# Down projection of expert tiles as three products of rounded parts, and table writes in bursts, in a perceiver layer with 64 experts

## The reference

```python
g = silu(einsum('ech,eih->eci', buf, expert_wg))
u = einsum('ech,eih->eci', buf, expert_wu)
out_buf = einsum('eci,ehi->ech', g * u, expert_wd)   # the down projection, i = 256, h = 512
rows = out_buf[e_flat, pos]
routed = (rows.reshape(T, K, h) * topw[..., None]).sum(1)
```

## Time and profile before

| | us |
|---|---|
| median of 3 runs | 1292.07 (1289.84 to 1292.19) |
| the profiled execution | 1291.37 |
| its span, first to last instruction | 1289.4 |
| TensorE busy in the span | 1225.0 (95%) |
| VectorE, ScalarE, GpSimd busy | 733.9, 594.8, 395.2 |
| stage B's item loop | from about 772 to 1268 |

### The profile page before, as it was taken

The page is one execution under the profiler, slowest core; times in us unless marked ns, Lnnn a source line. Parts: engine busy times, 40 slices in busy tenths (PEclk is TensorE's granted clock), DMA queues, the critical chain, the costliest instruction groups (busy, mean ns, idle before and its releaser), DMA issues. The chain is left out here.

```text
span 1289.4 us, 31822 instructions
## 1 busy us (share of the span) xinstructions
PE 1225.0 (95%) x9830; PEld 923.9 (72%) x9831; DVE 733.9 (57%) x1509; ACT 594.8 (46%) x1184; POOL 395.2 (31%) x312
## 2 busy tenths in 40 slices
PE   5999999999999999999999789999999999999993
PEld 4887788787887887877786347766777676667661
DVE  4445665756656657566557746556555556655550
ACT  2453433433434434333342165566655656656551
POOL 0002012021021120210202324566554656756442
PEclk9999999999999999999999999999999999999997
DMA  6732110210201102101012277999999999999886
GB/s 223 288 117 45 51 37 19 69 36 12 76 19 50 38 19 69 36 19 58 13 50 68 74 264 252 314 314 342 302 297 283 308 330 333 347 283 317 260 236 106
DMA packets 67370, 205.44 MB, mean 159 GB/s; under 512 B 16064, under 2 KB 18496, under 8 KB 56913
## 3 DMA queue, kind: packets, MB, share of 16 engines
q1 hardware_dynamic: 43392, 159.78, 34.3%
q0 software_dynamic: 23888, 44.40, 16.5%
HBM read 177.32 MB, written 37.03 MB: 166 GB/s over the span
## 5 line engine op out<-in xcount | busy, mean ns | idle before, releaser
L982 PE MATMUL bank<-ch,wkh 128*128 128x256 f32 x512 | 157.2, 307 | 11.9 <-DVE cl L660 8.4
L566 ACT ACTIVATE kt<-bank,colb 128x256 f32<-128x256 f32 x128 | 60.7, 474 | 225.7 <-PE bank L984 225.7
L459 POOL TENSOR_TENSOR rstd<-vep,half 128x1 f32<-128x1 f32 x32 | 20.7, 647 | 462.2 <-DVE vep L641 462.2
L1650 PE MATMUL ebank<-guh,xth 128*128 128x512 f32 x380 | 154.8, 407 | 1.5 <-DVE xtl L1548 0.8
L1543 DVE TENSOR_TENSOR gul<-wgu,guh 128x2048 fp32r<-128x2048 f32 x54 | 123.8, 2293 | 56.9 <-ACT guh L1459 56.8
L1387 POOL DMA_INDIRECT xg<-xn_rows,ig x95 | 123.4, 1299 | 89.8 <-issue 64.7
L1652 PE MATMUL ebank<-guh,xtl 128*128 128x512 f32 x380 | 149.0, 392 | 0.0
L1651 PE MATMUL ebank<-gul,xth 128*128 128x512 f32 x380 | 148.3, 390 | 0.0
L983 PE MATMUL bank<-cl,wkh 128*128 128x256 f32 x512 | 145.0, 283 | 0.0
L984 PE MATMUL bank<-ch,wkl 128*128 128x256 f32 x512 | 144.9, 283 | 0.0
L1680 PE MATMUL ebank<-wd,ht 128*128 128x512 f32 x292 | 134.3, 593 | 0.8 <-ACT ht L1444 0.8
(11 more groups left out here) (242 smaller groups left out, 2466.5 us busy)
## 6 DMA issues: line engine op xcount, KB each, us to landing
wgu<-in_egu SPq DMA_DIRECT2D x54, 1024.0 KB, 8.7
wd<-in_edn SPq DMA_DIRECT2D x54, 512.0 KB, 6.5
sgu<-in_egu SPq DMA_DIRECT2D x17, 1024.0 KB, 9.0
craw<-in_ctx SPq DMA_DIRECT2D x32, 514.0 KB, 3.3
sdn<-in_edn SPq DMA_DIRECT2D x17, 512.0 KB, 5.7
wqkv<-in_wqkv SPq DMA_DIRECT2D x1, 3072.0 KB, 18.1
second_sums<-x1b SPq DMA_DIRECT2D x9, 256.0 KB, 3.9
xa<-in_x SPq DMA_DIRECT2D x8, 256.0 KB, 3.0
```

Source lines behind the costliest of these rows:

```text
L982: mm(out, wkh[:, c, w], h[:, c, :], start=c == 0, stop=False)
L1650: mm(out, ah[:, c, :], bh[:, c, :], start=c == 0, stop=False)
```

## The change

In stage B the down projection is done with rounded parts too, over all of its 256 inner columns (`DS = 2` chunks of 128, which is all of `IC`).

- ScalarE's copy of the turned h (L1444) now rounds it (`hth`), and VectorE makes its remainder (`low_h`, 128x256), first thing in its step after the index copies.
- ScalarE rounds the down weights of item k (`high_d`, 128x1024) in step k between silu of k and the x cast of k+2; VectorE makes their remainder (`low_d`, 128x1024) at the end of step k, behind the gate-up remainder. Both have two buffers.
- TensorE's `down` waits for `d_low` and `hT_low` and does six products per tile instead of two plain ones.
- The turned h of the shared expert and a small scratch row move into buffers that exist already, and ScalarE waits once more ahead of its loop.

In stage A the eight table writes of a tile go one behind the other without pacing, ScalarE's passes are written out instead of looped, and 28 semaphore increments (`FILL`) stand at the end of its stage. The name `FILL` had held the value that closes masked scores; all of the mask is open here.

```diff
@@ -83,8 +83,7 @@
 KEEP = 3
 EARLY = K
 WRITE = 8
-PACE = ("v", "A3", "DEN1", "NUM1")
-PACED = K - 1 - len(PACE)
+FILL = 28
 
 
 def place(n, t):
@@ -476,7 +475,6 @@
                 if front and s == WRITE:
                     table_ready(t - 2)
                 if front and WRITE <= s < WRITE + K:
-                    wait(pool, s_kv, 6 * (BT * t + b) + k, tick)
                     write(s - WRITE)
 
             def on_pre(n, t):
@@ -511,18 +509,12 @@
                     pool.wait_ge(s_nb, NB)
                     residual(t + 1)
                 if n == "outproj":
-                    if type(t) is int and t == NT - 1:
-                        px_wait(pool, n, t)
-                        write(K - 1)
                     root(norm_post(t, 1))
                     root(norm_post(t, 2))
                 if n == "pos" and type(t) is int and t >= NT - 2:
                     table_ready(t)
-                    for j in range(EARLY if t == NT - 1 else PACED):
+                    for j in range(EARLY if t == NT - 1 else K):
                         write(j)
-                if n in PACE and type(t) is int and t == NT - 1:
-                    px_wait(pool, n, t)
-                    write(PACED + PACE.index(n))
 
             def on_shared(n, j, c):
                 pass
@@ -621,7 +613,9 @@
                     act.wait_ge(s_shT, j + 1)
                     nc.scalar.copy(sht[k], st_ps[:, 0:I].rearrange("p (c n) -> p c n", c=IC)).then_inc(s_shTc, 1)
 
-            passes(act, per_batch, on_post, on_pre, on_shared, written_out=3)
+            passes(act, per_batch, on_post, on_pre, on_shared, written_out=NT - 3)
+            for _ in range(FILL):
+                act.sem_inc(tick, 1)
 
         @block.vector
         def _(dve):
...
@@ -1235,10 +1229,14 @@
-        row, run = sb("row", [1, 7, P]), sb("run", [1, 3, P])
+        row, run = sb("row", [1, 7, P]), tiles[1].ys[2][0:1, 0:3 * P].rearrange("a (r n) -> a r n", r=3)
+        wdh, wdl = ([sb(f"wd{n}{i}_", [P, DS, D], F32R) for i in range(2)] for n in "hl")
+        for tile in tiles:
+            tile.hth, tile.htl = (sb(f"h{n}{tile.half}_", [P, DS, P], F32R) for n in "hl")
+        sht = [tiles[1].ys[j][:, 0:I].rearrange("p (c n) -> p c n", c=IC) for j in range(2)]

@@ -1441,7 +1439,7 @@
                 done(act, tile, "hT", item)
-                nc.scalar.copy(tile.ht[:, :, :], ht_ps[tile.half][:, 0:IC * P].rearrange("p (c n) -> p c n", c=IC)).then_inc(tile.s["hT_copied"], 1)
+                nc.scalar.copy(tile.hth[:, :, :], ht_ps[tile.half][:, 0:IC * P].rearrange("p (c n) -> p c n", c=IC)).then_inc(tile.s["hT_copied"], 1)
 
@@ -1457,6 +1455,11 @@
                 nc.scalar.copy(guh[par][:, :, :], wgu[w][:, :, :]).then_inc(s_w["gu_high"], 1)
+
+            def high_d(item):
+
+                act.wait_ge(s_wd[item.w], (item.wturn + 1) * 16)
+                nc.scalar.copy(wdh[item.par][:, :, :], wd[item.w][:, 0:DS, :]).then_inc(s_w["d_high"], 1)
 
@@ -1515,12 +1518,17 @@
             act.wait_ge(s_ss, 16 * SHB)
+            act.wait_ge(d.s_kept, 16 * (SHA - KEEP))
 
             def part_of(it, part):
                 its = items(act, it, part - 1, 7, TAB2)
                 for k in range(part, part + 4):
                     halves(act, its[k - 1], h_turned)
-                    halves(act, its[k], silu)
+                    with act.If(its[k].valid):
+                        silu(its[k], tiles[0])
+                        with act.If(its[k].two):
+                            silu(its[k], tiles[1])
+                        high_d(its[k])
                     halves(act, its[k + 2], turned)
@@ -1541,6 +1549,17 @@
                 V.tensor_tensor(gul[par][:, :, :], wgu[w][:, :, :], guh[par][:, :, :].bitcast(F32), ALU.subtract).then_inc(s_w["gu_low"], 1)
+
+            def low_d(item):
+
+                w_done(dve, "d_high", item)
+                V.tensor_tensor(wdl[item.par][:, :, :], wd[item.w][:, 0:DS, :], wdh[item.par][:, :, :].bitcast(F32), ALU.subtract).then_inc(s_w["d_low"], 1)
+
+            def low_h(item, tile):
+
+                done(dve, tile, "hT_copied", item)
+                V.tensor_tensor(tile.htl[:, :, :], ht_ps[tile.half][:, 0:DS * P].rearrange("p (c n) -> p c n", c=DS),
+                                tile.hth[:, :, :].bitcast(F32), ALU.subtract).then_inc(tile.s["hT_low"], 1)
 
@@ -1634,10 +1653,13 @@
                         scatter_rows(its[k - 1])
+                    halves(dve, its[k - 1], low_h)
                     halves(dve, its[k], hidden)
                     halves(dve, its[k + 2], low_x)
                     with dve.If(its[k + 2].valid):
                         low_gu(its[k + 2].i, its[k + 2].w, its[k + 2].par)
+                    with dve.If(its[k].valid):
+                        low_d(its[k])
 
@@ -1675,9 +1697,12 @@
                 done(pe, tile, "y_ready", item, 1)
-                done(pe, tile, "hT_copied", item)
-                for c in range(IC):
-                    last = mm(y_ps[tile.half][:, :], tile.ht[:, c, :], wd[item.w][:, c, :], start=c == 0, stop=c == IC - 1)
+                w_done(pe, "d_low", item)
+                done(pe, tile, "hT_low", item)
+                for c in range(DS):
+                    last = split_mm(y_ps[tile.half][:, :], tile.hth, tile.htl, wdh[item.par], wdl[item.par], c, IC)
+                for c in range(DS, IC):
+                    last = mm(y_ps[tile.half][:, :], tile.ht[:, c - DS, :], wd[item.w][:, c, :], start=False, stop=c == IC - 1)
                 last.then_inc(tile.s["down"], 1)
```

More of the change, by code:

```diff
@@ L1182 @@
 NR = 2 * JB
+DS = 2
 class Tile:
@@ L1199, in __init__ @@
         self.xtl = [sb(f"xtl{i}_", [P, DC, P], F32R) for i in range(2)]
-        self.ht = sb("ht_", [P, IC, P])
         self.sg, self.h = sb("sg_", [P, I]), sb("h_", [P, I])
         self.s_g = [sem(f"rows_in{i}_") for i in range(NX)]
-        names = ("xT", "xT_high", "xT_low", "gu", "silu", "h_ready", "hT", "hT_copied", "down", "y_ready")
+        names = ("xT", "xT_high", "xT_low", "gu", "silu", "h_ready", "hT", "hT_copied", "hT_low", "down", "y_ready")
         self.s = {n: sem(n + "_") for n in names}
@@ L1252, in stage_b @@
         s_go, s_gone = sem("scatter_begun"), sem("gather_begun")
-        s_w = {n: sem(n) for n in ("gu_high", "gu_low")}
+        s_w = {n: sem(n) for n in ("gu_high", "gu_low", "d_high", "d_low")}
         tick = sem("tick_b")
@@ L1482, in shared_ht @@
                     act.wait_ge(s_sd, j - 1)
-                nc.scalar.copy(tiles[j % 2].ht[:, :, :], xt_ps[j % 2][:, 0:I].rearrange("p (c n) -> p c n", c=IC)).then_inc(s_shTc, 1)
+                nc.scalar.copy(sht[j % 2], xt_ps[j % 2][:, 0:I].rearrange("p (c n) -> p c n", c=IC)).then_inc(s_shTc, 1)
             def blank(xg):
@@ L1709, in shared_down @@
                 for c in range(IC):
-                    last = mm(sd_ps[j % 2][:, :], tiles[j % 2].ht[:, c, :], sdn[:, c, :], start=c == 0, stop=c == IC - 1)
+                    last = mm(sd_ps[j % 2][:, :], sht[j % 2][:, c, :], sdn[:, c, :], start=c == 0, stop=c == IC - 1)
                 last.then_inc(s_sd, 1)
```

## The result

| | before | after |
|---|---|---|
| median of 4 runs | 1291.92 us (1289.84 to 1292.19) | 1363.08 us (1351.76 to 1366.59) |
| profiled execution, span | 1291.37, 1289.4 | 1363.98, 1362.2 |
| mean granted clock, as a share of full speed | 0.991 | 0.967 |
| item loop, first gate-up to end | 772.6 to 1267.7: 495.1 | 769.5 to 1340.0: 570.5 |

The change makes the kernel slower: ratio 1.0539, 95% interval 1.0501 to 1.0578, 71 us. The forecast was 1330 us and the range ended at 1348. Its direction and its main mechanism hold; its sum was 33 us short.

The account below looks back on a forecast made before the run. TensorE was taken to bound the kernel. Stalls +64.5, register loads +6, TensorE's saving -26 and old waits -6 gave +38.5 us on the profiled 1291.37: 1330 us, range 1306 to 1348.

Parts of the forecast that it names:

- What bounds the kernel: Expert loop: TensorE, busy 490.25 of 496 us, is the bound; only shortening its stream can win.
- TensorE's saving: Down projections: six rounded products take 1.47 us for 1.72 (single), 2.84 for 3.44 (double); 26 us saved.
- Sizes of the three new instructions: ScalarE's down-weight rounding 1.05 us; VectorE's down-weight remainder 1.22 and remainder of h 0.42.
- The new wait: TensorE's down projection waits for h's remainder: chain 7.6 us against 5.07, 2.5 per full stall, 29 stalls, 64.5 us.
- Register loads: VectorE's item-field loads show behind its added work in half of 18 rounds, 0.7 us each: 6 us.
- The clock: Rival, 10%: new TensorE stalls lower the granted clock in the loop, adding 13 to 26 us, middle 19: 1349.
- all 29 stalls would pay: Clock case by the skill's page: every stall in the expert loop sends the clock back, 38 us or more.
- the casts hide: Rival, 5%: ScalarE and VectorE do the new work in idle time, only TensorE's saving counts: 1265 us.
- only VectorE's sum counts: Rival, 5%: VectorE's total work in single steps, TensorE's in double ones, sets the loop: 1280 us.
- The 6 us of old waits: TensorE's idle in the expert loop, mostly late weights and register loads, vanishes under the longer steps: 6 us less.

Follow-up runs that it names:

- products-only run: Changed kernel with the down weights' parts and the remainder of h made once ahead of the loop: 1272.88 us, ratio 0.9848.
- both moves: Changed kernel with ScalarE's down-weight rounding ahead of silu and VectorE's down-weight remainder ahead of the gate-up remainder: 1300.04 us, ratio 1.0067.
- second profile: The same changed kernel run again on another chip, profiled at a clock of 0.977: 1361.39 us, ratio 1.0548.
- filler in front of single items: Changed kernel plus one overwritten f32 product ahead of the down projection where the next item is single: 1355.06 us, ratio 1.0511.
- halved: Changed kernel with both moves and the gate-up remainder in two halves, the remainder of h between in three of four steps: 1362.08 us, ratio 1.054.

## Why the prediction was wrong

- **What bounds the kernel** held. TensorE did; now the chain from ScalarE to VectorE does.
- **TensorE's saving,** 26 us forecast, was 31.8. The down projection has its forecast length (1.47 a single, 2.81 to 2.85 a double for 2.84), but each starts 0.08 us sooner behind the turning of x, 5.7 us in all; the prediction kept 0.43 for that turning. The products-only run shows the saving net of small losses.
- **Sizes of the three new instructions** and their places: within 0.01 us.
- **The new wait.** Chain 7.7 us (7.6), full stall 2.5, every other single. All stalls ahead of down projections are 62.4 us more than before, for 64.5 + 6 forecast with VectorE's register loads. VectorE's own idle time at these loads is 9.7 us in 17 places, 0.9 at most, close to the 6 us forecast. Right in mechanism, and 8 us too large. Order is what costs: with both moves 40 us of these stalls go. By the Trainium skill's "TensorE: Matmul & The Clock Gate", section "Architectural detail: the array is 16× 32×32, not 1× 128×128", the vector queues are first in, first out; the traces agree, with the remainder of h at 907.63 behind everything of its step though its source, written 904.57 to 904.96, had been ready for 2.7 us.
- **Register loads: the step that failed.** I asked where VectorE's would be seen and gave them 6 us. TensorE's own, 18 in the loop of 1.9 to 3.0 us (one of 4.2 in the second profile), I gave nothing, because before they cost next to nothing. They were hidden by the lead of TensorE's queue, which the new wait takes. They show 13 us after the change and 20 in the second profile, for under 2 before. In all, the turning of h starts 24 to 27 us later in sum, 13 to 15 of it in phases with a slow stretch. The filler in front of single items, with no low clock there, leaves 19.6 (23.5 - 3.9), and the profile's own idle time ahead of the turning is 15.7. The exposed loads come with the wait: 2.5 us of idle time without it, 5.7 with 17 us of stall. Beyond that they don't grow with the stalls: eight other kernels, fillers aside, have 10.9 to 18.4 with 19 to 63 of stall, and *halved* has 6.6 with 59.
- **Ahead of gate-ups** 5.3 us more: 15 late starts of some 0.6 for 10 before. It is 4.2 more even with the products alone; the cause of that I have not shown.
- **The clock.** I gave its fall 10% and a price of 13 to 26 us on top, and none in the sum. It fell in fact, 16 and 10 stretches in the two loops, mostly behind idle times of TensorE of some 2 us and more (of 16 and 17 of 2.0 to 2.8 us in the two profiles, 9 and 8 lie at a fall). The Trainium skill's same page, section "HAM oscillation — how this bites in real kernels", tells of a kernel whose returning idle times send the clock back every time. The traces agree that it happens, and not that it happens each time. That all 29 stalls would pay was my own step: the section's kernel has longer gaps. The run with the filler puts the cost at 5 us, and the spread between runs at up to 10. I had looked at the one fall behind 4.37 us and taken shorter gaps to be safe.
- **Rivals.** That the casts hide, and that only VectorE's sum counts, were both refuted: 32 us of saving come with 62 of stall. VectorE stands at 67% of the loop.

By sum, in the profiled loop: take the 38.5 forecast, less 5.8 for more saving and 8.1 for less stall. The 6 us of old waits come back on, since the table's differences leave them out already. With the 44.7 us (23.8 + 5.3 + 15.6) of the three places that had no term it is 75.3. Too small a saving and too large a stall made the forecast 14 us longer and so hid part of what was missing, which is luck. Of the 44.7 the loads are 11, the gate-ups 5; the other 28 lie mostly in phases with a slow stretch. In the second profile it is 18, 6 and 16. How much of that rest the clock caused is not shown beyond the 5 and 10 us above.

## What to carry to other kernels

When a wait is added to an engine that was never late, price three things: the wait, the register loads and branches that its queue did ahead of time until then, and what the idle does to the clock. Work that is moved off a full engine should be laid by the order in which its results are wanted, not by where it is easy to append: the changed kernel is 5.4% slower than the one before, and 0.7% with the two weight instructions a place earlier on their engines. Where an instruction of 2.3 us stands before a short one that others wait for, halving it is worth a try: here it brought 1.0% more (from 0.7% slower to 0.3% faster), and cost 4.7% where the loop had grown too long.

## What the runs showed of the hardware

- A register load in the item loop held TensorE's queue for 1.9 to 4.2 us (18 in each of two profiles, most of them 1.9 to 2.6). Before the change 16 of 18 were hidden, with the queue some 2 us ahead of its engine; after it 6 and 3 were.
- In *halved*, VectorE's loop shows 85 packets in the instruction queue for 25, and eight idle times of 6.8 to 7.9 us with no releaser, one at each jump back of its loop.
- The granted clock fell to 1.2 GHz behind idle times of 1.7 to 3.1 us, not behind each of them (one of 2.96 passed without a fall), and the loop of the same kernel had 16 falls in one profile and 10 in another.
